# A decoder layer's cross-attention output projection, moved from unit 3's second gap to unit 4's first

## What is computed

```
x = _layernorm(x + attn(x, Wq, bq, Wk, bk, Wv, bv, Wo, bo))          # 16 heads of 16, ALiBi bias
x = _layernorm(x + xattn(ctx, ctx, x, mask, cWq, ..., cWo, cbo))      # keys and values from ctx
x = _layernorm(x + ffn(x, gate_w, w1, b1, w2, b2))                    # top 2 of 8 experts
```

## Time and profile before

| | us |
|---|---|
| median of 3 runs | 1416.11 (1415.9 to 1416.43) |
| the profiled execution | 1412.27 |
| its span | 1410.2 |
| PE busy | 1091.7 (77%) |
| DVE busy | 1022.0 (72%) |
| ACT busy | 567.4 (40%) |
| POOL busy | 483.5 (34%) |

### The profile page before, as it was taken

The page is one execution under the profiler, slowest core; times in us unless marked ns, Lnnn a source line. Parts: engine busy times, 40 slices in busy tenths (PEclk is TensorE's granted clock), DMA queues, the critical chain, the costliest instruction groups (busy, mean ns, idle before and its releaser), DMA issues. The chain is left out here.

```text
span 1410.2 us, 32514 instructions
## 1 busy us (share of the span) xinstructions
PE 1091.7 (77%) x9874; PEld 772.1 (55%) x9875; DVE 1022.0 (72%) x2410; ACT 567.4 (40%) x1022; POOL 483.5 (34%) x597
## 2 busy tenths in 40 slices
PE   3778899889888888888885600088999999999980
PEld 2445666666655655565553400066777777777750
DVE  2579999999888989999985340066777777777764
ACT  1344555555545656665563200022323323332324
POOL 1233433433344343534322037612223223223324
PEclk7799999999999999999997555599999999999995
DMA  8489886678756887788754152275222222222227
GB/s 207 108 225 226 230 200 142 157 180 227 174 108 163 235 237 154 207 232 221 202 168 137 68 194 106 100 267 159 42 43 43 41 45 41 41 45 41 43 30 245
DMA packets 160383, 202.20 MB, mean 143 GB/s; under 512 B 30444, under 2 KB 141692, under 8 KB 157067
## 3 DMA queue, kind: packets, MB, share of 16 engines
q1 hardware_dynamic: 145864, 182.92, 48.7%
q0 software_dynamic: 13296, 17.83, 7.5%
q10 hardware_dynamic: 1152, 0.53, 0.2%
HBM read 122.63 MB, written 74.41 MB: 140 GB/s over the span
## 5 line engine op out<-in xcount | busy, mean ns | idle before, releaser
L1177 PE MATMUL HB<-xhi,W 128*128 128x128 f16 x2272 | 292.1, 221 | 21.7 <-issue 16.1
L1177 PEld LDWEIGHTS HB<-xhi,W 128*128 x2272 | 202.2, 98 | 65.8 <-issue 48.2
L1177 PE MATMUL HB<-xlo,W 128*128 128x128 f16 x1136 | 225.0, 220 | 0.0
L1460 POOL DMA_INDIRECT d_sums<-ysc,tok x71 | 111.0, 1563 | 327.3 <-DMA XB<-d_rows 171.7
L892 ACT ACTIVATE PT<-SB 128x1024 f32<-128x1024 f32 x128 | 131.1, 1024 | 138.3 <-PE SB L563 136.3
L659 DVE TENSOR_REDUCE mneg<-SA 128x4 f32<-128x1024 f32 x128 | 156.5, 1223 | 41.6 <-PE SA L515 39.5
L1177 PEld LDWEIGHTS HB<-xlo,W 128*128 x1136 | 111.9, 99 | 50.2 <-issue 0.7
L1370 DVE SCALAR_TENSOR_TENSOR hlo<-HB,hhi 128x512 f16<-128x512 f32 x142 | 98.2, 691 | 55.1 <-ACT hhi L1238 51.1
L1238 ACT ACTIVATE hhi<-HB 128x512 f16<-128x512 f32 x142 | 84.2, 593 | 121.3 <-DVE HB L1362 121.2
L1362 DVE SCALAR_TENSOR_TENSOR HB<-HB,SC,b1c 128x512 f32<-128x512 f32 x142 | 107.1, 754 | 16.7 <-PE HB L1177 11.9
L1246 ACT ACTIVATE ysc<-yb,wv 128x256 f32<-128x256 f32 x71 | 36.1, 508 | 191.8 <-DVE yb L1394 181.6
(11 more groups left out here) (195 smaller groups left out, 2500.4 us busy)
## 6 DMA issues: line engine op xcount, KB each, us to landing
wst<-in_w SPq DMA_DIRECT2D x32, 1024.0 KB, 10.0
d_w<-w SPq DMA_DIRECT2D x16, 1024.0 KB, 6.7
W<-d_w SPq DMA_DIRECT2D x8, 2048.0 KB, 8.7
k_stack<-d_k SPq DMA_DIRECT2D x96, 128.0 KB, 7.2
XB<-d_rows SPq DMA_DIRECT2D x71, 130.0 KB
d_rows<-fill SPq DMA_DIRECT2D x4, 1950.0 KB, 15.6
d_q<-q_part SPq DMA_DIRECT2D x16, 384.0 KB, 5.8
d_k<-k_part SPq DMA_DIRECT2D x16, 384.0 KB, 2.7
```

The source lines that it names most:

```text
L1177: mm = pe.matmul(out, w.rearrange("p e n -> p (e n)"), x[n % 2][:, k, :], start=(k == 0 and half == 0 and x is xhi), stop=(k == KT - 1 and ...
L1460: pool.indirect_dma_start(YS, bass.IndirectOffsetOnAxis(ap=tok[n % 6][:, 0:1], axis=0), ysc[n % 2][:, :], None, compute_op=ALU.add).then_i ...
```

## The change

The entry for `Oc` in `GAPS` goes from (3, 1) to (4, 0), with the same batch offset.

```diff
-            (2, 1): ("AOTc", -2), (3, 0): ("K", 1), (3, 1): ("Oc", -2), (4, 1): ("Kc", 0),
+            (2, 1): ("AOTc", -2), (3, 0): ("K", 1), (4, 0): ("Oc", -2), (4, 1): ("Kc", 0),
```

## The result

The changed kernel takes 1434.3 us, the median of three executions, against 1416.0 for the kernel before; the ratio is 1.0131, with a 95% interval of 1.0091 to 1.0171. A fourth execution took 1880 us at a mean granted clock of 0.55, where the others had 0.90 to 0.91, and is in neither number. The profiled execution took 1434.33 us, with a span of 1432.4. In a later group of runs it took 1435.45 against 1418.5 (1.0131, 1.0103 to 1.0159). So it is slower by 1.3%, some 17 to 18 us.

A forecast was written before the change was run, and what follows sets the result against it. PE waits for the `cq_stack` DMA before unit 4's scores, and the projection fills that wait. -0.5 + 3.2 + 6.6 + 2.7 = 12.0 us on 1412.27, plus 3.8 to the median: 1428 us, range 1417.5 to 1437.

The forecast's parts named there:

- The read of `cq_stack` is the gate: Ahead of unit 4's scores on PE: they wait for this DMA, 6.3 to 7.1 us after its first issue.
- S: The start of the scores of unit 4 on PE, claimed to stay at about 313.48 us in the steady step.
- The rival in which S moves forward: Unit 4's scores follow PE's transpose, not the read, and the projection fills the hole: -14 us, 1402; chance 0.12.
- The order on PE: Units 4 to 5, 14 steps: projection behind unit 4's scores, unit 5's scores 5.80 us after them; -0.5 us.
- Step 16, +3.2 us: Step without self attention: the projection leaves the DMA's wait, L712 comes at 775.2 against 771.95, later units wait; +3.2 us.
- The clock, +6.6 us for four falls: PE idle ahead of unit 4's scores: new clock falls in steps 2, 7, 14 and 15, 1.65 us each; eight at most.
- the threshold from the earlier trace: PE idle times of 1.85 us and more were followed by a clock fall, those up to 1.61 us were not.
- The rival of no new falls: Clock around unit 4: the three old falls go and none come; 1418.8 to 1424 us; chance 0.18.
- The port, +2.7 us of 0 to 5.3: Five early steps without a fall: POOL's `x1bo` may hold DVE's copy into `cq_stack` 1.1 us; half taken.
- the three old falls: Clock falls in steps 9, 10 and 13 of the kernel before, claimed to go; 1.7 us won each.
- The sum, 12.0 us: Whole kernel: order -0.5, step 16 +3.2, clock +6.6, port +2.7; forecast 1428 us.
- the rival with eight falls: Clock around unit 4: 1.7 us idle is enough and step 8 falls too; 6.6 us more, 1435; chance 0.12.

The follow-up runs named there:

- `filler_short`: The changed kernel with six transposes put ahead of the scores of unit 4 and POOL's `x1bo` cut to 8 columns; 1418.9 us, 1.0016 of the kernel before.
- `short_before`: The kernel before, with POOL's `x1bo` cut to 8 of 256 columns per token row; 1415.4 us, 0.9982 of the kernel before.
- the filler: Six transposes of the identity ahead of the scores of unit 4, added to the changed kernel; alone 1426.5 us, 1.0056 of the kernel before.
- the cut: POOL's `x1bo` reduced to 8 of 256 columns per token row; alone in the changed kernel 1432.0 us, 1.0101 of the kernel before.
- `hybrid`: The kernel before with the `Oc` entry moved to (4, 0) in steps 9 to 15 only; 1416.1 us, 0.9981 of the kernel before.
- `pe40_dve41`: The changed kernel with DVE's addition and statistics in unit 4's second gap; 1421.2, 1422.6, 1441.3 and 1441.5 us, 1.0112 of the kernel before.

## Why the prediction was right, point by point

- **The read of `cq_stack` is the gate.** Right. S stood 6.3 to 6.8 us after the issue in all 14 steps of the changed kernel, PE idled 1.3 us or more ahead of it, and the wait was put down to the read each time. The rival in which S moves forward fell.
- **The order on PE: `keyed` at S + 2.26, the scores of unit 5 at S + 5.80, in sum -0.5 us.** Right where the clock held: 2.20 and 5.75. With both other causes taken away, 3.8 us are left (`filler_short` against `short_before`), where -0.5 and 3.2 were forecast for the order and step 16; the noise of such a difference is of the same size, so the -0.5 is neither confirmed nor refuted.
- **Step 16, +3.2 us.** The delay of the chain was right: the scores of unit 5 came 3.5 us later. What it cost was 1.6 us in the changed kernel and 3.6 in `filler_short`. "Every later unit waits in turn" holds where the clock stays low; the forecast left out that it can rise behind the projection and give half back.
- **The clock, +6.6 us for four falls, 13.2 as the bound.** That falls at S would come and cost about 1.6 us each was right. Taking the falls away measured 8.9 us with the port collision in place and 13.1 without; the term was 2.3 us or more too small. In the two traces of the changed kernel the three falls at S lengthened the way to the scores of unit 5 by 4.8 and 6.2 us together, and step 8, which the sum left out, by 2.3 and 2.6 (8.04 and 8.31 us, against 5.75 with the filler). What failed is the threshold from the earlier trace rows. (The idle times that the forecast worked out, redone from the trace of the kernel before, are 1.4 to 1.6, 1.7 to 1.8 and 1.9 to 2.6 us, a little more than it said.) In the five traces with the projection behind S in all these steps and no filler (steps 2 to 15 without 8), the clock fell in 4 of 23 steps with 1.3 to 1.6 us idle ahead of S, in 3 of 17 with 1.6 to 1.8, in 7 of 11 with 1.8 to 2.1 and in 7 of 12 above (two more, below 1.2 us, had none); step 2 of the first trace idled 2.55 us and had no fall. In these counts it is a chance that is larger above 1.8 us than below, and other steps are struck in each execution; it isn't a limit. Of the named steps 2, 7, 14 and 15, one had a fall in the first trace and three in the second. And the forecast looked only at the idle time ahead of S, not at the one that a held copy makes.
- **The rival of no new falls**, which was also what the Trainium skill, "TensorE: Matmul & The Clock Gate", section "Why this matters for your kernels", would have. The measurement decides against it for this kernel: falls followed idle times from 1.41 us on, and filling part of this time was worth 9 us.
- **The port, +2.7 us of 0 to 5.3.** The two starts were within 0.1 us in steps 2 to 6, as said, and POOL was first in all seven early steps, those with a fall too, which the sum had left out. Half of a coin was taken where one outcome came each time; and two terms were missing, the later holds in unit 5 (L708, 1.18 us above) and the falls behind the wait. By the times the size is less sure: the cut brought 3.5 us in one pair and 7.7 in the other, and 3.4 in the kernel before, so the port's own part is between nothing and 4.3 us, and the 2.7 lies within that. The Trainium skill's "GPSIMD Engine Reference", section "Key points", names contention with DVE instructions that have two SBUF inputs or run in a 2-port mode. The trace agrees for L708, which has two inputs (1.18 against 0.17 us); the copy has one and was held too (1.51 against 0.42), and no trace shows its mode.
- **Gains of the late steps.** The sum took the three old falls as cured, and both traces of the changed kernel have none in steps 9, 10 and 13. But by `hybrid` the late steps gain 3 us at most in the median of many executions; its trace shows one fall that came elsewhere.

The sum, 12.0 us, came out 5 to 6 us low: the change measured 17.0 us in the second group and 18.3 in the first. Port and clock together were priced at 9.3 us and measured 13.2 (1435.5 less 1418.9, less the 3.4 of `short_before`); the rest was priced at 2.7 and measured 3.8. The time lies within the stated range, but at the upper end of the 1422 to 1434 that was given for four falls. It is near the 1435 of the rival with eight falls, by chance: the traces had three falls at S each, and the port and step 8 made up the rest. What stays open: how port and clock share the 13.2 us, why the clock falls in one step and not in another of like idle time, and what made two executions of `pe40_dve41` 20 us longer than the other two.

## What to carry to other kernels

Before an operation is moved off an engine's path, look at what else the engine would wait for there: here it filled the time of a DMA, so moving it only changed which side of the wait it stood on. Where two engines must both do a part of an item, move them apart: PE's and DVE's parts together lost 17 us, DVE's part alone gained 4, and 7 in the late steps only. And an operation that is held by a port where its engine is covered can be held one unit later where another engine waits for it, so each shift of POOL's work needs a look at what DVE does 0.1 us behind it.

## What the runs showed of the hardware

- Six useless transposes inside a wait made the kernel 8.9 us faster (1435.45 to 1426.52), and no step of that trace had a fall at S.
- Idle times of PE of 1.3 to 1.6 us ahead of S were followed by a fall of the clock in 4 of 23 cases, the shortest of the four being 1.41 us; above 1.8 us in 14 of 23 (five traces).
- A DVE copy of 15 partitions (0.42 us) took 1.51 us behind a POOL addition that had started 0.03 us earlier; subtractions of 128x8 took 1.18 and 1.26 us in place of 0.17.
- In step 16, behind a projection of 3.73 us at the low clock, the granted clock rose; it was 0.67 in the mean up to the last router result in the changed kernel, against 0.50 before, and 1.6 us were lost where the chain had been delayed by 3.5. In `filler_short` it was 0.54, and 3.6 us were lost.
